# A graph network kernel on one core: the column norms are masked by GpSimd, and VectorE's scaling and mask become one operation

## The chip, the cores and the metric

The kernel runs on one core of a Trainium2 chip. The metric is the device time of one execution, in microseconds (us); lower is better. The median of three runs of the kernel before is 1269.06 us (1268.77 to 1270.68).

## What is computed

The reference, cut to what matters here (128 graphs of 128 nodes with 512 features; `adj` is a 128 by 128 matrix of zeros and ones with ones on its diagonal):

```python
h = relu(layernorm(x))
z_l, z_g, v = h @ W_lang.T, h @ W_grav.T, h @ W_V.T
zn  = z_l / max(norm(z_l), EPS)
A_l = max(zn @ zn.T, 0) * not_eye
A_g = exp(-d2(z_g) / (2 * sigma**2)) * not_eye
K   = w_l * rows_sum_to_one(A_l * adj) + (1 - w_l) * rows_sum_to_one(A_g * adj)
x   = x + (K @ v) @ W_O.T
h   = relu(layernorm(x))
x   = x + (adj * adj).T @ h + bias        # per graph, over the nodes
```

In the second layer the nodes are mixed by the elementwise square of `adj`, and a bias is added to every row. What matters for the change is `A_l`: each raw similarity S[n, m] is multiplied by the reciprocal norm of column m, cut off at zero, and multiplied by mask[n, m] = adj[n, m] without the diagonal. The row's own norm comes in later, in the row factors.

## The kernel before, in words

The 128 graphs are taken in 32 groups of four (`GB` = 4). Every engine has its own instruction stream, and the streams are tied by semaphores; within an engine the order is the one written out in its `iteration` function. Nothing reorders it: an engine that waits holds back everything behind it. All products are made of three passes over high and low parts of fp32 numbers, so for each operand ScalarE writes a high part (`y_hi`, `v_hi`, `h_hi`, `hT_hi`) and VectorE or GpSimd subtracts it to get the low part (`y_lo`, `v_lo`, `h_lo`, `hT_lo`).

One iteration i of TensorE is, in order: eight y blocks (products of the turned h with `Lw`, into four PSUM banks called `ring` used in turn), with the transposes of K of group i-1 before the eighth (L879); four K times v products of group i-1; four P products (`p_ps`); four v products, with the transposes of P after the third (L939); and four second-layer products of group i-1, each of three matmuls (`ring<-h_hi,A_hi`, `h_lo,A_hi`, `h_hi,A_lo`), each of which waits for its `h_lo` (`h2_split`). A product may only start when the bank it writes has been drained (`free`).

VectorE's iteration (`iteration` of the vector block): low parts of the eight y blocks, and between them the mask of the second similarity (`mask_g`), the row factors (L602 to L611), the block transposes of the next h, `combine` and `kt_lo` (L622) of group i-1; then the residual additions and statistics (L631, L637, L568), the squared norms (`squared_norms`, L753, L757 and last L759, which writes `sqc`); then for b = 0 to 3 the low part of v (L557) and that of the turned h of the next group (`turned_lo`, L576), with the sum L744 after b = 2; then the four outputs of group i-1 (L688), which free the ring banks for the next y blocks; then `similarities` (L586: the sums times the column norms) and `mask_l` (L592: cut off at zero, times the mask).

GpSimd's iteration: the ten small operations of `norm1(i+1)` (L277 to L291); `add_bias` of group i-1 for b = 0 and 1 (L301); `norm2(i-1)` (the same ten lines); `add_bias` for b = 2 and 3; `row_norms(i)` (L314 writes `rn` from `sqc`, L316 writes `wr`); and `h2_lo(i-1)` for b = 0 to 3 (L308, writes `h_lo`, after ScalarE's `h_hi`).

SyncE waits for the first operation of `row_norms` and then issues two transfers (`spread_norms`): L214 writes `rn` to a small DRAM tensor, and when that has landed L216 reads it back to all partitions as `rn_cols`, 128 x (128 x 4), with the group's four graphs innermost. VectorE reads it with m innermost, which is a step of four elements.

The last group (i = 31) has no `spread_norms`; its column norms come through PSUM (`r_ps`).

Of the kernel before, what the change touches and what calls it, by code (L numbers as in the profile page):

```python
# [5 lines left out]
ALU = mybir.AluOpType  # L6
# [5 lines left out]
P = 128  # L12
Q = 32
GB = 4
# [6 lines left out]
def gnn_pair(nc, x, adj, w_lang, w_grav, w_v, w_o, gate_logit, log_sigma, bias, out):  # L21
# [6 lines left out]
    LN_STEPS = 10  # L28
    LAST_STEPS = 7
    RN_STEPS = 2  # L30
    blk = {ac: n for n, ac in enumerate(TRI)}
    NQ = P // Q
    TURN = 16 * NQ * NQ
# [20 lines left out]
    with ExitStack() as ctx:  # L54
# [3 lines left out]
        def sem(name):  # L58
            return ctx.enter_context(nc.semaphore(name))
# [10 lines left out]
        P_sb, diag, A = (chain[:, n] for n in range(3))  # L70
# [9 lines left out]
        mask = sb("mask", [P, P])  # L80
# [17 lines left out]
        rn_cols = sb("rn_cols", [P, P, GB])  # L98
# [24 lines left out]
        r_ps = ctx.enter_context(nc.psum_tensor("r_ps", [P, GB, P], F32))  # L123
        kt_ps = ctx.enter_context(nc.psum_tensor("kt_ps", [P, GB, P], F32))

        def bank(use):
# [12 lines left out]
        rn_stored, rn_spread = sem("rn_stored"), sem("rn_spread")  # L139
# [6 lines left out]
        pt_done, r_done, kt_done, kv_done, l1_done = (  # L146
            sem("pt_done"), sem("r_done"), sem("kt_done"), sem("kv_done"), sem("l1_done"))
# [8 lines left out]
        s_ready = sem("s_ready")  # L156
        sq_ready = sem("sq_ready")
        a_ready = sem("a_ready")
# [10 lines left out]
        h2_done = sem("h2_done")  # L169
        x2b_ready = sem("x2b_ready")  # L170
        diag_ready = sem("diag_ready")
        rn_step = sem("rn_step")

        def passes(hi_lo_lhs, hi_lo_rhs):

# [24 lines left out]
        def _(sp):  # L200
# [10 lines left out]
            def spread_norms(g):  # L211

                sp.wait_ge(rn_step, RN_STEPS * g + 1)
                sp.dma_start(rn_dram, rn[:, 0]).then_inc(rn_stored, 16)  # L214
# [47 lines left out]
        def _(pool):  # L262
# [34 lines left out]
            def add_bias(g, b):  # L297
                if b == 0:
                    wait_for(pool, out_stored, 16 * GB * g)
                pool.wait_ge(bn2_done, GB * g + b + 1)  # L300
                pool.tensor_tensor(x_out[:, b], x_rows(g, b), bias_sb[:, :], ALU.add).then_inc(x2b_ready, 1)  # L301

            def norm2(g):
                std_factors(g, bn2, bn2_done, ln2, ln2_step)

# [5 lines left out]
            def row_norms(g):  # L311
                pool.wait_ge(sq_ready, 3 * g + 3)
                wait_for(pool, k_ready, g)
                pool.tensor_tensor(rn[:, 0], sqc[:, :], neg_half[:, :], ALU.pow).then_inc(rn_step, 1)  # L314
                pool.wait_ge(rn_step, RN_STEPS * g + 1)
                pool.tensor_tensor(wr[:, :, :], rn_lg, w8[:, :, :], ALU.mult).then_inc(rn_step, 1)  # L316

            def iteration(i, before=True, after=True):
                if after:
                    norm1(i + 1)  # L320
                if before:
                    for b in range(GB // 2):
                        add_bias(i - 1, b)
                    norm2(i - 1)
                if not after:
                    row_norms(i)
                if before:
                    for b in range(GB // 2, GB):
                        add_bias(i - 1, b)
                if after:  # L330
                    row_norms(i)
                if before:
                    for b in range(GB):
                        h2_lo(i - 1, b)

            norm1(0)
# [7 lines left out]
            g = NG - 1  # L344
# [205 lines left out]
        def _(dve):  # L550
# [25 lines left out]
                dve.tensor_tensor(hT_columns(1, b), h_columns(b), part(hT_columns(0, b)), ALU.subtract)\  # L576
                   .then_inc(ht_lo, 1)

            def similarities(g, last=False):
                if last:  # L580
                    dve.wait_ge(r_done, 1)
                else:
                    dve.wait_ge(rn_spread, 16 * g + 16)
                dve.wait_ge(s_ready, g + 1)
                by_col = r_ps[:, :, :] if last else rn_cols[:, :, :].rearrange("p m b -> p b m")
                dve.tensor_tensor(A[:, :, 0], A[:, :, 0], by_col, ALU.mult).then_inc(a_ready, 1)  # L586

            maskb = mask[:, :].unsqueeze(1).to_broadcast([P, GB, P])

            def mask_l(g):  # L590
                dve.wait_ge(a_ready, 3 * g + 1)
                dve.scalar_tensor_tensor(out=A[:, :, 0], in0=A[:, :, 0], scalar=0.0, in1=maskb,  # L592
                                         op0=ALU.max, op1=ALU.mult).then_inc(a_ready, 1)

# [3 lines left out]
                                         op0=ALU.min, op1=ALU.mult).then_inc(a_ready, 1)  # L598

            def row_factors(g):  # L600
                dve.wait_ge(a_ready, 3 * g + 3)
                dve.tensor_reduce(deg[:, 0], A, AX.X, ALU.add).then_inc(deg_step, 1)  # L602
                dve.wait_ge(deg_step, 5 * g + 1)
                dve.tensor_tensor(deg[:, 1], deg[:, 0], rn_lg, ALU.mult).then_inc(deg_step, 1)
                dve.wait_ge(deg_step, 5 * g + 2)
                dve.tensor_scalar(deg[:, 1], deg[:, 1], EPS, None, ALU.max).then_inc(deg_step, 1)
                dve.wait_ge(deg_step, 5 * g + 3)
                dve.reciprocal(deg[:, 2], deg[:, 1]).then_inc(deg_step, 1)
                dve.wait_ge(deg_step, 5 * g + 4)
                dve.wait_ge(rn_step, RN_STEPS * (g + 1))  # L610
                dve.tensor_tensor(deg[:, 3], deg[:, 2], wr[:, :, :], ALU.mult).then_inc(deg_step, 1)  # L611
# [69 lines left out]
            def h2_lo(g, b):  # L681
                dve.wait_ge(h2_hi, GB * g + b + 1)
                dve.tensor_tensor(h2[1][:, b], h2f[:, b], part(h2[0][:, b]), ALU.subtract).then_inc(h2_split_dve, 1)
# [6 lines left out]
            def iteration(i, before=True, after=True, stats=True):  # L690
                n = 0
                hi = first_hi(i)
                for a in range(C):
                    for l in range(2):
                        hi = hi + 1
                        lo(y[1][:, a, :, l], bank(n).rearrange("p (b m) -> p b m", b=GB), y[0][:, a, :, l], hi)\
                            .then_inc(drained, 1)
                        n += 1
                        if not before and n <= 2:
                            factor_lo(C + 2 * n - 2)  # L700
                            factor_lo(C + 2 * n - 1)
                        if before and n == 1:
                            mask_g(i - 1)
                        if before and n == 2:
                            row_factors(i - 1)
                        if after and n == 4:
                            turn_blocks(i + 1, 0)
                            turn_blocks(i + 1, 1)
                        if before and n == 4:
                            combine(i - 1)  # L710
                        if after and n == 5:
                            turn_blocks(i + 1, 2)
                            turn_blocks(i + 1, 3)
                        if before and n == G_USES - 1:
                            kt_lo(i - 1)
                if before:
                    residual(i - 1, n, first_use(i) + n, i + 2 if stats and after else None)
                else:
                    for c in range(C):
                        hi += 1  # L720
                        lo(MT[1][:, c], bank(n + c), MT[0][:, c], hi).then_inc(drained, 1)
                    x_stats(i + 2, 0, GB)
                n += GB
                if not after:
                    last_chain(i, n, hi)
                    return
                squared_norms(i)
                for b in range(GB):
                    hi = hi + 1
                    lo(v[1][:, b], bank(n), v[0][:, b], hi)\  # L730
                        .then_inc(drained, 1 if before or b < GB - 1 else 1 + GB)
                    n += 1
                    turned_lo(i + 1, b)
                    if b == 2:
                        sum_s(i)
                if before:
                    for b in range(GB):
                        output(i - 1, b, n + b)
                similarities(i)
                mask_l(i)  # L740

            def sum_s(g):
# [18 lines left out]
            def last_chain(i, n, hi):  # L761
                squared_norms(i)

                def v_lo(b):
                    lo(v[1][:, b], bank(n + b), v[0][:, b], hi + b + 1).then_inc(drained, 1)

                v_lo(0)
                sum_s(i)
                similarities(i, last=True)
                mask_l(i)  # L770
                mask_g(i)
                row_factors(i)
                for b in range(1, GB - 1):
                    v_lo(b)
                combine(i)
                v_lo(GB - 1)
                for b in range(GB):
                    output(i - 1, b, n + GB + b)
                    if b == 0:
                        kt_lo(i)  # L780
# [61 lines left out]
            g = NG - 1  # L842
# [165 lines left out]
```

## Time and profile before

| | us |
|---|---|
| median of 3 runs | 1269.06 |
| profiled execution, its own time | 1269.61 |
| its span, first to last instruction | 1267.7 |
| TensorE busy | 1241.2 (98%) |
| VectorE busy | 1058.5 (83%) |
| ScalarE busy | 694.5 (55%) |
| GpSimd busy | 574.7 (45%) |
| granted TensorE clock, mean | 0.996 of full |

In the profile PE is TensorE, DVE is VectorE, ACT is ScalarE, POOL is GpSimd and SPq is SyncE's queue. The shares are means over the span; which wait ends last in a stretch has to be read from the timeline. A matmul's record is longer than the distance to the next matmul, because they are pipelined.

### The profile page before, as it was taken

The numbers are of one execution on the slowest core, as the hardware profiler recorded it, in microseconds if no ns is written. First come the engines' busy times: TensorE is split into PE (matmuls) and PEld (weight loads), VectorE is DVE, ScalarE is ACT, GpSimd is POOL, SyncE is SP. The second block draws the span as 40 slices with busy tenths as digits, with TensorE's granted clock in tenths as the row PEclk, the third lists the DMA queues.
The fourth block names the chain that finished last, engine by engine and source line by source line (L and its number), as shares of the span: only waits on it lengthen the run. The fifth ranks groups of instructions, "written<-read, shape, count | busy, mean of one in ns | idle before, by whom it ended". The sixth has DMA issues, their size and how long they took to land.

```text
span 1267.7 us, 22572 instructions
## 1 busy us (share of the span) xinstructions
PE 1241.2 (98%) x6324; PEld 1039.6 (82%) x6324; DVE 1058.5 (83%) x1826; ACT 694.5 (55%) x1324; POOL 574.7 (45%) x964
## 2 busy tenths in 40 slices
PE   7999999999999999999999999999999999999996
PEld 6878888888888888888888888888888888888884
DVE  5678888988888988888898888898888898888777
ACT  5346555456645456655446655546655545654543
POOL 1115553434554434554434555444555443455433
PEclk9999999999999999999999999999999999999998
DMA  6232424342333343333343232344242444243201
GB/s 243 34 72 81 106 54 95 99 108 81 102 71 78 99 108 87 95 79 70 99 108 97 86 93 56 99 108 103 79 108 49 99 101 108 79 103 69 47 34 66
DMA packets 308894, 112.55 MB, mean 89 GB/s; under 512 B 269840, under 2 KB 269968, under 8 KB 308880
## 3 DMA queue, kind: packets, MB, share of 16 engines
q1 hardware_dynamic: 177360, 95.78, 27.2%
q10 hardware_dynamic: 131520, 16.60, 7.9%
q8 instruction: 7, 0.11, 0.0%
q14 instruction: 7, 0.06, 0.0%
HBM read 46.20 MB, written 33.62 MB: 63 GB/s over the span
## 4 chain that ended last, share of the span: by engine, by line
PE 93%; DVE 4%; ACT 1%; issue 1%; DMA 1%; POOL 0%; SPq 0%; DVEq 0%; ACTq 0%
PE ring L866 75%; PE p_ps L866 15%; PE p_ps L939 2%; PE kt_ps L879 1%; DMA h2f<-in_L_gnn_W_grav 1%; DVE x_out L688 0%; DVE bn L568 0%; DVE y_lo L557 0%; ACT h L379 0%; DVE bn L637 0%; DVE x_ring L631 0%; DVE y_lo L784 0%; DVE deg L602 0%; DVE v_lo L784 0%; DVE hT_lo L557 0%
## 5 line engine op out<-in xcount | busy, mean ns | idle before, releaser
L301 POOL TENSOR_TENSOR x_out<-x_ring,bias_sb 128x512 f32<-128x512 f32 x128 | 162.8, 1295 | 499.9 <-DVE bn L637 499.9
L866 PE MATMUL ring<-hT_hi,Lw_hi 128*128 128x512 f32 x640 | 256.9, 401 | 4.9 <-DVE hT_lo L576 2.1
L406 ACT ACTIVATE y_hi<-ring 128x512 fp32r<-128x512 f32 x256 | 148.3, 592 | 206.5 <-PE ring L866 203.7
L866 PE MATMUL ring<-hT_hi,Lw_lo 128*128 128x512 f32 x640 | 250.6, 392 | 0.0
L866 PE MATMUL ring<-hT_lo,Lw_hi 128*128 128x512 f32 x640 | 250.2, 391 | 0.0
L866 PE MATMUL ring<-MT_hi,hT_hi 128*128 128x512 f32 x512 | 203.0, 396 | 0.0
L557 DVE TENSOR_TENSOR v_lo<-ring,v_hi 128x512 fp32r<-128x512 f32 x128 | 88.5, 692 | 136.8 <-ACT v_hi L442 136.8
L866 PE MATMUL ring<-MT_hi,hT_lo 128*128 128x512 f32 x512 | 200.0, 391 | 0.0
L866 PE MATMUL ring<-MT_lo,hT_hi 128*128 128x512 f32 x512 | 199.9, 390 | 0.0
L308 POOL TENSOR_TENSOR h_lo<-h2f,h_hi 128x512 fp32r<-128x512 f32 x124 | 158.0, 1296 | 84.8 <-ACT h_hi L476 84.8
L557 DVE TENSOR_TENSOR y_lo<-ring,y_hi 128x512 fp32r<-128x512 f32 x256 | 169.2, 680 | 28.4 <-ACT y_hi L406 28.3
L430 ACT ACTIVATE chain<-p_ps 128x512 f32<-128x512 f32 x64 | 38.2, 598 | 240.5 <-PE p_ps L866 240.5
L866 PEld LDWEIGHTS ring<-hT_hi,Lw_hi 128*128 128x128 f32 x640 | 120.2, 188 | 44.0 <-DVE x_out L688 10.7
L866 PE MATMUL p_ps<-y_hi,hT_lo 128*128 128x256 f32 x512 | 145.2, 284 | 0.0
L866 PE MATMUL p_ps<-y_lo,hT_hi 128*128 128x256 f32 x512 | 145.2, 284 | 0.0
L866 PE MATMUL p_ps<-y_hi,hT_hi 128*128 128x256 f32 x512 | 145.0, 283 | 0.0
L866 PEld LDWEIGHTS ring<-hT_hi,Lw_lo 128*128 128x128 f32 x640 | 120.2, 188 | 26.4
L866 PEld LDWEIGHTS ring<-hT_lo,Lw_hi 128*128 128x128 f32 x640 | 120.5, 188 | 21.8
L469 ACT ACTIVATE h2f<-x_ring,ln 128x512 f32 (+1 forms) x128 | 100.5, 809 | 49.6 <-POOL ln L291 40.0
L866 PEld LDWEIGHTS ring<-MT_hi,hT_lo 128*128 128x128 f32 x512 | 96.2, 188 | 20.6
L866 PEld LDWEIGHTS ring<-MT_lo,hT_hi 128*128 128x128 f32 x512 | 96.5, 188 | 17.9
L866 PEld LDWEIGHTS ring<-MT_hi,hT_hi 128*128 128x128 f32 x512 | 96.4, 188 | 18.0
(160 smaller groups left out, 2537.0 us busy)
## 6 DMA issues: line engine op xcount, KB each, us to landing
x_ring<-in_x SPq DMA_DIRECT2D x32, 1024.0 KB, 5.5
out<-x_out SPq DMA_DIRECT2D x128, 256.0 KB, 2.2
h_turned<-h SPq DMA_DIRECT2D x248, 64.0 KB, 2.1
h_turned<-h ACTq DMA_DIRECT2D x248, 64.0 KB, 2.1
rn_cols<-rn_dram SPq DMA_DIRECT2D x31, 256.0 KB, 3.9
x_ring<-in_L_gnn_W_lang SPq DMA_DIRECT2D x4, 256.0 KB, 5.6
h2f<-in_L_gnn_W_grav SPq DMA_DIRECT2D x1, 1024.0 KB, 9.2
chain<-in_L_gnn_W_O SPq DMA_DIRECT2D x1, 1024.0 KB, 13.0
```

Of the source, the lines that this page charges most:

```text
L301: pool.tensor_tensor(x_out[:, b], x_rows(g, b), bias_sb[:, :], ALU.add).then_inc(x2b_ready, 1)
L308: pool.tensor_tensor(h2[1][:, b], h2f[:, b], h2[0][:, b].bitcast(F32), ALU.subtract)\
L406: act.activation(y[0][:, a, :, l], bank(n).rearrange("p (b m) -> p b m", b=GB), ACT.Copy)\
L430: act.activation(P_sb[:, 2 * half:2 * half + 2], p_ps[:, 2 * half:2 * half + 2], ACT.Copy)\
L469: act.activation(h2f[:, b], x_rows(g, b), ACT.Relu, bias=ln2[:, SHIFT, b:b + 1], scale=ln2[:, RSTD, b:b + 1]).then_inc(h2_done, 1)
L557: return dve.tensor_tensor(out, ps, part(hi), ALU.subtract)
L866: mm = pe.matmul(out, lhsT, rhs, start=(k == 0), stop=(k == len(terms) - 1))
L879: mm = pe.transpose(kt_ps[:, b], K[:, b], ident[:, :])
L939: mm = pe.transpose(p_ps[:, k // 2, k % 2], P_sb[:, k // 2, k % 2], ident[:, :])
```

## The change

`mask_norms(g)` is new on GpSimd: it waits until `rn_cols` of the group has landed and multiplies it by the mask in place (4 graphs innermost, so the mask is read with a step of zero there). On VectorE `similarities` is gone, and `mask_l` does the cut at zero and the multiplication by the masked norms in one operation. GpSimd's order changes: `row_norms(i)` goes ahead of the second pair of `add_bias`, `h2_lo` for b = 0 and 1 follows that pair, then `mask_norms(i)`, then `h2_lo` for b = 2 and 3. The last group keeps the two operations, in a function of their own, and its GpSimd order.

```diff
+            def mask_norms(g):
+                pool.wait_ge(rn_spread, 16 * g + 16)
+                by_col = mask[:, :].unsqueeze(2).to_broadcast([P, P, GB])
+                pool.tensor_tensor(rn_cols[:, :, :], rn_cols[:, :, :], by_col, ALU.mult).then_inc(rn_masked, 1)
+
...
-                if not after:
-                    row_norms(i)
+                row_norms(i)
                 if before:
                     for b in range(GB // 2, GB):
                         add_bias(i - 1, b)
+                    for b in range(GB // 2):
+                        h2_lo(i - 1, b)
                 if after:
-                    row_norms(i)
+                    mask_norms(i)
                 if before:
-                    for b in range(GB):
+                    for b in range(GB // 2, GB):
                         h2_lo(i - 1, b)
...
-            def similarities(g, last=False):
...
-                dve.tensor_tensor(A[:, :, 0], A[:, :, 0], by_col, ALU.mult).then_inc(a_ready, 1)
...
             def mask_l(g):
-                dve.wait_ge(a_ready, 3 * g + 1)
+                dve.wait_ge(rn_masked, g + 1)
+                dve.wait_ge(s_ready, S_STEPS * (g + 1))
+                dve.scalar_tensor_tensor(out=A[:, :, 0], in0=A[:, :, 0], scalar=0.0,
+                                         in1=rn_cols[:, :, :].rearrange("p m b -> p b m"),
+                                         op0=ALU.max, op1=ALU.mult).then_inc(a_ready, 1)
...
             def row_factors(g):
-                dve.wait_ge(a_ready, 3 * g + 3)
+                dve.wait_ge(a_ready, 2 * g + 2)
...
-                similarities(i)
                 mask_l(i)
```

## Rows read from the trace of the kernel before

**Rows 1.** The page: busy time of each engine, share of the span, instructions.

```profile
PE 1241.2 (98%) x6324; PEld 1039.6 (82%) x6324; DVE 1058.5 (83%) x1826; ACT 694.5 (55%) x1324; POOL 574.7 (45%) x964
```

**Rows 2.** Waits, whole span: who waited for whom, us in total, times, longest.

```profile
PEld ring L866 <- issue: 16.9, 31, 2.5
```

**Rows 3.** Timeline of PE in one iteration: start us, us, instruction, count.

```profile
617.33 0.39 PE L866 MATMUL ring<-hT_hi,Lw_lo 128*128 128x512 f32 x1
617.79 0.49 PE L866 MATMUL ring<-v_hi,KT_hi 128*128 128x512 f32 x1
618.12 0.39 PE L866 MATMUL ring<-v_lo,KT_hi 128*128 128x512 f32 x1
...
640.25 0.39 PE L866 MATMUL ring<-h_hi,A_hi 128*128 128x512 f32 x1
...
641.02 0.50 PE L866 MATMUL ring<-hT_hi,Lw_hi 128*128 128x512 f32 x1
```

**Rows 4.** Timeline of DVE in the same iteration; in brackets the idle time before.

```profile
604.94 1.07 DVE L586 TENSOR_TENSOR chain<-chain,rn_cols 128x512 f32<-128x512 f32 x1
...
606.65 0.68 DVE L557 TENSOR_TENSOR y_lo<-ring,y_hi 128x512 fp32r<-128x512 f32 x1
...
616.98 0.67 DVE L622 TENSOR_TENSOR KT_lo<-kt_ps,KT_hi 128x512 fp32r<-128x512 f32 x1
618.39 0.69 DVE L557 TENSOR_TENSOR y_lo<-ring,y_hi 128x512 fp32r<-128x512 f32 x1 [0.73 <-ACT y_hi L406]
...
626.22 0.67 DVE L753 TENSOR_TENSOR chain<-chain,diag_of 128x512 f32<-128x512 f32 x1
...
628.97 0.69 DVE L759 TENSOR_SCALAR sqc<-sq 128x4 f32<-128x4 f32 x1
...
631.17 0.68 DVE L576 TENSOR_TENSOR hT_lo<-h_turned,hT_hi 128x512 fp32r<-128x512 f32 x1
...
634.38 0.82 DVE L576 TENSOR_TENSOR hT_lo<-h_turned,hT_hi 128x512 fp32r<-128x512 f32 x1
...
636.09 0.68 DVE L576 TENSOR_TENSOR hT_lo<-h_turned,hT_hi 128x512 fp32r<-128x512 f32 x1
...
639.04 0.69 DVE L557 TENSOR_TENSOR v_lo<-ring,v_hi 128x512 fp32r<-128x512 f32 x1 [1.14 <-ACT v_hi L442]
639.65 0.72 DVE L576 TENSOR_TENSOR hT_lo<-h_turned,hT_hi 128x512 fp32r<-128x512 f32 x1
640.29 2.47 DVE L688 TENSOR_TENSOR x_out<-ring,x_out 128x512 f32<-128x512 f32 x4
```

**Rows 5.** Timeline of POOL in the same iteration; the row at 633.35 is the second of its pair.

```profile
604.11 0.20 POOL L287 TENSOR_TENSOR ln<-ln 128x4 f32<-128x4 f32 x1
...
626.23 0.72 POOL L287 TENSOR_TENSOR ln<-ln 128x4 f32<-128x4 f32 x1
...
628.34 2.55 POOL L301 TENSOR_TENSOR x_out<-x_ring,bias_sb 128x512 f32<-128x512 f32 x2
630.83 1.04 POOL L314 TENSOR_TENSOR rn<-sqc,neg_half 128x4 f32<-128x4 f32 x1
...
632.10 2.56 POOL L308 TENSOR_TENSOR h_lo<-h2f,h_hi 128x512 fp32r<-128x512 f32 x2
...
633.35 1.31 POOL L308 TENSOR_TENSOR h_lo<-h2f,h_hi 128x512 fp32r<-128x512 f32 x1
...
637.27 2.55 POOL L308 TENSOR_TENSOR h_lo<-h2f,h_hi 128x512 fp32r<-128x512 f32 x2 [2.61 <-ACT h_hi L476]
```

**Rows 6.** DMA issues, whole span: queue, count, KB each, median us to landing.

```profile
rn_cols<-rn_dram SPq DMA_DIRECT2D x31, 256.0 KB, 3.9
...
rn_dram<-rn SPq DMA_DIRECT2D x31, 2.0 KB, 1.4
```

**Rows 7.** Timeline of DVE in the first group.

```profile
63.34 0.17 DVE L759 TENSOR_SCALAR sqc<-sq 128x4 f32<-128x4 f32 x1
```

**Rows 8.** Timeline of POOL in the first group.

```profile
63.59 1.01 POOL L314 TENSOR_TENSOR rn<-sqc,neg_half 128x4 f32<-128x4 f32 x1 [27.03 <-DVE sqc L759]
```

More of the change, by code:

```diff
@@ L30, in gnn_pair @@
     RN_STEPS = 2
+    S_STEPS = 1
     blk = {ac: n for n, ac in enumerate(TRI)}
@@ L171, in gnn_pair @@
         diag_ready = sem("diag_ready")
-        rn_step = sem("rn_step")
+        rn_step, rn_masked, a_scaled = sem("rn_step"), sem("rn_masked"), sem("a_scaled")
         def passes(hi_lo_lhs, hi_lo_rhs):
@@ L577, in turned_lo, with mask_l_last @@
                    .then_inc(ht_lo, 1)
-            def similarities(g, last=False):
[L580 to L585, printed above, removed]
-                dve.tensor_tensor(A[:, :, 0], A[:, :, 0], by_col, ALU.mult).then_inc(a_ready, 1)
             maskb = mask[:, :].unsqueeze(1).to_broadcast([P, GB, P])
             def mask_l(g):
-                dve.wait_ge(a_ready, 3 * g + 1)
+                dve.wait_ge(rn_masked, g + 1)
[3 more added lines that the diff above has]
+                                         op0=ALU.max, op1=ALU.mult).then_inc(a_ready, 1)
+            def mask_l_last(g):
+                dve.wait_ge(r_done, 1)
+                dve.wait_ge(s_ready, S_STEPS * (g + 1))
+                dve.tensor_tensor(A[:, :, 0], A[:, :, 0], r_ps[:, :, :], ALU.mult).then_inc(a_scaled, 1)
+                dve.wait_ge(a_scaled, 1)
                 dve.scalar_tensor_tensor(out=A[:, :, 0], in0=A[:, :, 0], scalar=0.0, in1=maskb,
@@ L768, in last_chain @@
                 sum_s(i)
-                similarities(i, last=True)
-                mask_l(i)
+                mask_l_last(i)
                 mask_g(i)
```

## The prediction

> **What bounds the kernel now.** I read the page first: TensorE is busy 98% of the span [rows 1]. VectorE, from which the change takes work, is busy 83%, and GpSimd, which gets it, 45% [rows 1]. From shares one would call the change harmless and nearly useless. So the question is what is left of TensorE's idle time, and who ends it. The waits [rows 2] name one place that comes 31 times, once a group, with 16.9 us of idle time in all, whose end the profile puts down to "issue". The timeline of TensorE [rows 3] places it. At 617.33 the last matmul of the y blocks starts and the next one, the first of K times v, only at 617.79, where the pace is 0.23 us; VectorE's low part of K ends at 616.98 + 0.67 = 617.65 [rows 4], 0.14 before the start, so this is the true releaser. The matmul after that comes 0.33 later, not 0.23. The stall is thus 0.23 + 0.10 = 0.33 us. A second place is the head of the y blocks, 641.02, just after the first output is drained: 640.29 + 0.68 = 640.97 (four outputs take 2.47, so 0.60 each after the first of 0.68) [rows 3, 4].
>
> Two things are then to be seen in the other engines' timelines. VectorE has no idle time from 604.94 until after the low part of K, so work taken from it there brings that forward; after it VectorE waits for ScalarE (618.39, bracket), which waits for TensorE, and its timing from there on hangs on TensorE's y blocks alone [rows 4]. And GpSimd and VectorE hold each other up. The small sqc operation takes 0.17 in the first group, where GpSimd is waiting for it [rows 7, 8]; here it takes 0.69: it starts at 628.97 and ends at 629.66, when GpSimd's first bias sum (628.34 plus about 1.29) ends [rows 4, 5]. The low part of turned h at 634.38 takes 0.82 and not 0.68: GpSimd's operation ends at 633.35 + 1.31 = 634.66, VectorE's at 635.20, 0.54 later. In the other direction, a GpSimd operation on 128x4 that started at 626.23, beside VectorE's L753 (626.22 to 626.89), took 0.72 and ended 0.06 after it; the same line in norm1 took 0.20 [rows 4, 5]. Operations of VectorE that read PSUM (L557, L688) show none of this.
>
> **The change, part by part.**
>
> *VectorE's operation that goes.* From the start of L586 to the next y_lo are 1.71 us (604.94 to 606.65) for the two operations [rows 4]. The fused one reads the same rn_cols with the same step of four elements, so I take the 1.07 of L586; the row does not exclude the 0.69 of the operation without that step, nor 1.07 plus a few hundredths. VectorE saves about 0.6 us an iteration. The low part of K then ends near 617.05, before TensorE's 617.56, and the stall of 0.33 goes. What is late next decides its worth. TensorE comes 0.33 earlier to its last v product, ScalarE's v_hi and VectorE's v_lo start at 638.71 and not 639.04, and the last turned low part (L576) wants to start at 639.32. But it reads two operands in SBUF, and GpSimd's last h_lo runs until 637.27 + 2.55 = 639.82. By the 0.54 above it ends at 640.36, the first output at 640.96, where it ended at 640.97. So without any change on GpSimd, the 0.33 is given back at the next y block: gain 0.0 us.
>
> *Row norms moved ahead of two bias sums.* With the row norms next, GpSimd only waits from 628.34 on, so sqc is not held up: 628.97 + 0.17 = 629.14. L314 starts 0.08 later (63.51 to 63.59 [rows 7, 8]), at 629.22, and SyncE's L214 about 1.05 later, at 630.27, 1.6 us earlier than now. Then 1.4 and 3.9 us to the landings [rows 6]: rn_cols is there at 635.6 to 636.1. SyncE itself has nothing else queued there: its outputs and x loads wait for later events. The first bias sum of the pair starts at 629.22 + 1.27 = 630.49 (L314 to the next long operation is 1.27, 630.83 to 632.10 [rows 5]).
>
> *The new operation on GpSimd.* No row shows a multiplication there with a step of zero. The nearest rows are 128x512 sums of 1.29 us, at a pitch of 1.25 [rows 5]; I take 1.29. Above, VectorE's ratio for its strided operand, 1.07 to 0.69, would give 2.0 us; below, 1.25.
> The Trainium skill (GPSIMD Engine Reference, section 7, Performance pitfalls) puts a surcharge of about half on GpSimd reads whose step exceeds 8 bytes. The steps here are 4 and 0 bytes, so the page speaks for 1.29; no row shows it.
>
> *Price of a collision.* When VectorE wants an operation of two SBUF operands during a long GpSimd operation, it starts 0.14 before that one's end is recorded and ends 0.54 after it. The next GpSimd operation then starts 0.14 before VectorE's end, so 0.40 after its predecessor's end, and not 0.04 before it (632.10 + 1.29 against 633.35 [rows 5]): 0.44 us for each collision. In the trace of before every collision falls on the last operation of a GpSimd pair, with idle time behind it, so nothing is lost. After the change GpSimd has seven long operations in a row:
>
> - bias sum 2: 630.49 to 631.78; turned low part 0 wants 631.17: collision
> - bias sum 3: 632.18 to 633.47
> - h_lo 0: 633.43 to 634.72; turned low part 1 wants 634.38: collision
> - h_lo 1: 635.12 to 636.41; turned low part 2 wants 636.09: collision
> - mask of the norms: 636.81 to 638.10 (rn_cols is there, no wait for it)
> - h_lo 2: 638.06 to 639.35; turned low part 3 wants 639.32, at its very end
> - h_lo 3: if VectorE gets in first, 639.75 to 641.04; if not, 639.31 to 640.60.
>
> TensorE wants h_lo 3 at 640.25, less the 0.33 [rows 3]. In the first branch it starts 0.14 after 641.04, loses 0.11 at the restart and takes 3 x 0.227: the y blocks are in pace at 641.97. Before, that was 641.02 + 0.11 = 641.13. So +0.84 an iteration. In the second branch h_lo 3 allows 641.53, but turned low part 3 ends at 640.60 + 0.54 = 641.14, the first output at 641.74, the y blocks are in pace at 641.90: +0.77. I take 0.81. norm1 on GpSimd, behind h_lo 3, is then 0.8 to 1.3 us later, against y blocks that are 0.8 later too; its first reader is ScalarE after the third y_hi, so I cost it at nothing. If that cover were gone, up to 0.5 us an iteration would come on top.
>
> *The sum.* mask_norms runs for 31 groups, with h_lo behind it in 30: 30 x 0.81 = 24.3 us. The first group has no h_lo behind its mask, and the last keeps its order: 0. The profiled execution is 1269.61 with a span of 1267.7, 0.04% above the median of 1269.06: 1269.1 + 24.3 = 1293.4 us.
>
> At this place a page can be weighed. The rows give 0.44 for a collision. The Trainium skill (SBUF — State Buffer, The single rule and Practical consequences) says that the shared port pair is held for the whole instruction by whichever starts first, and that the other fully blocks. By that a collision would cost GpSimd a full operation of VectorE. The trace agrees that they block, but its blocked operations end 0.54 and not 0.68 after the other.
>
> **The rivals.**
>
> *Not slower (12%).* GpSimd is not delayed by VectorE when its next long operation is already queued; only short operations show such a delay now. Then the row is 630.49, 631.74, 632.99, 634.24 to 635.53, the mask 635.65 to 636.94, and h_lo 2 and 3 start at 637.27 after ScalarE as now: 1269 us, since the 0.33 is given back as worked out. It decides at a mask ending by 637.3. Against it: sqc, wanted at 628.97, got in between two long operations [rows 4, 5].
>
> *Faster (8%).* As the last, and turned low part 3 is not held up either: first output at 640.60, h_lo 3 at 639.82, y blocks in pace at 640.07 + 0.68 = 640.75, so 0.38 less an iteration, 1257.7 us. Against it stands the 0.82 of the low part at 634.38 [rows 4].
>
> *One collision fewer (12%).* The mask ends at 637.66, h_lo 3 at 640.16, turned low part 3 at 640.70, the first output at 641.30 against 640.97: +0.33 x 30, 1279 us. The ends lie 0.3 us from the collisions' edges, so this is possible.
>
> *A longer mask or longer holds (18%).* With 2.0 us for the mask, h_lo 3 ends at 641.74 and the y blocks are in pace at 642.67: +1.54 x 30, 1315 us. With 0.68 a collision (VectorE's usual duration, at 631.17 [rows 4]), three cost 0.72 more: h_lo 3 ends about 641.8, 1316 us.
> The second of these is what the rule on the shared port pair (the Trainium skill, SBUF — State Buffer) would give.
>
> **How the numbers follow.** The forecast's own case has 50%, by its rows of 1290 to 1298 us. Slower cases together 80%, unchanged 12%, faster 8%. A measurement of this kernel tells 0.2% (2.5 us) from no change. The range goes from the unchanged case to the longer mask: 1268 to 1316 us; it leaves out the faster case and what a still slower mask would bring.
>
> **What would show it.** Right: L759 at 0.17 us; L214 about 12 us after the eighth y_lo; KT_lo no longer the releaser of K times v; the low parts L576 at 0.9 to 1.3 us for b = 0 to 2; TensorE waiting for POOL h_lo in 30 iterations, 1 us or so each; a period of 38.55 and not 37.74. Wrong: h_lo 2 still waiting for ScalarE's h_hi, the mask beginning after a long wait for the DMA, or L301 and L308 unstretched while L576 is.

## The result, and the profile after

The changed kernel takes 1285.2 us (median of 4 runs, 1284.56 to 1285.99) against 1269.1 us for the kernel before on the same chip: ratio 1.0125, interval 1.0107 to 1.0142, slower by 16.1 us. The profiled execution took 1285.48 us, with a span of 1283.7. The forecast was 1293.4, in a range of 1268 to 1316.

The page of the changed kernel, busy time by engine, answers to [rows 1]. VectorE's busy time went up by 12 us although it has 31 operations fewer, and GpSimd's by 73 us for 31 more of about 1.1 us each, 34 us of work. The rest is time in which the two engines hold each other up: the profile counts an instruction as busy while it is held, as the longer records below show. So a busy share that rose is not work that was added.

```profile
PE 1248.2 (97%) x6324; PEld 1040.5 (81%) x6324; DVE 1070.9 (83%) x1795; ACT 691.7 (54%) x1324; POOL 647.8 (50%) x995
```

The waits of the whole span, against [rows 2]: who waited for whom, us in total, times, longest. The stall that the profile calls issue comes 59 times and not 31. It has also moved: before K times v it is gone, and it now stands before the second-layer products of b = 2 and b = 3 (the weight loads ahead of them wait 0.34 and 0.72 us on average). And there is a new line: TensorE waits for GpSimd's h_lo once in nearly every group.

```profile
PEld ring L872 <- issue: 33.0, 59, 2.5
PEld ring L872 <- DVE x_out L696: 16.1, 29, 0.6
...
PE ring L872 <- POOL h_lo L314: 9.3, 31, 0.8
```

TensorE's timeline in one iteration, against [rows 3] (start us, us, instruction, count). The K times v products now begin 0.23 after the last y product, at 626.12: that stall is gone. The second-layer products for b = 2 and 3, at 609.60 and 610.84, do not follow at the pace of 0.68 but 1.24 apart, and the y blocks start 0.52 after the last matmul.

```profile
609.29 0.39 PE L872 MATMUL ring<-h_hi,A_lo 128*128 128x512 f32 x1
609.60 0.49 PE L872 MATMUL ring<-h_hi,A_hi 128*128 128x512 f32 x1
...
610.84 0.49 PE L872 MATMUL ring<-h_hi,A_hi 128*128 128x512 f32 x1 [0.29 <-POOL h_lo L314]
...
611.40 0.40 PE L872 MATMUL ring<-h_hi,A_lo 128*128 128x512 f32 x1
611.92 0.50 PE L872 MATMUL ring<-hT_hi,Lw_hi 128*128 128x512 f32 x1
...
625.89 0.39 PE L872 MATMUL ring<-hT_hi,Lw_lo 128*128 128x512 f32 x1
626.12 0.39 PE L872 MATMUL ring<-v_hi,KT_hi 128*128 128x512 f32 x1
```

GpSimd's timeline from there to the next head, against [rows 5]. Both pairs of long operations now take 3.00 us and not 2.55, and the mask 1.56.

```profile
637.69 1.01 POOL L320 TENSOR_TENSOR rn<-sqc,neg_half 128x4 f32<-128x4 f32 x1 [0.87 <-DVE sqc L766]
...
638.97 3.00 POOL L302 TENSOR_TENSOR x_out<-x_ring,bias_sb 128x512 f32<-128x512 f32 x2
641.93 3.00 POOL L314 TENSOR_TENSOR h_lo<-h2f,h_hi 128x512 fp32r<-128x512 f32 x2
644.89 1.56 POOL L307 TENSOR_TENSOR rn_cols<-rn_cols,mask 128x512 f32<-128x512 f32 x1
646.41 2.53 POOL L314 TENSOR_TENSOR h_lo<-h2f,h_hi 128x512 fp32r<-128x512 f32 x2
```

VectorE's timeline of the same time, against [rows 4]. sqc is down to 0.17 us; the four turned low parts (L583) take 1.17, 0.91, 0.91 and 1.67 us where they took 0.68, 0.82, 0.68 and 0.72; and the first output, 649.42 to 650.11, is again what the next y block waits for. The last low part is the one that matters most: wanted at 647.83, while h_lo 3 runs until 648.94, it ends at 649.50.

```profile
637.44 0.17 DVE L766 TENSOR_SCALAR sqc<-sq 128x4 f32<-128x4 f32 x1
...
639.64 1.17 DVE L583 TENSOR_TENSOR hT_lo<-h_turned,hT_hi 128x512 fp32r<-128x512 f32 x1
...
642.87 0.91 DVE L583 TENSOR_TENSOR hT_lo<-h_turned,hT_hi 128x512 fp32r<-128x512 f32 x1
...
644.57 0.91 DVE L583 TENSOR_TENSOR hT_lo<-h_turned,hT_hi 128x512 fp32r<-128x512 f32 x1
...
647.83 1.67 DVE L583 TENSOR_TENSOR hT_lo<-h_turned,hT_hi 128x512 fp32r<-128x512 f32 x1
649.42 2.47 DVE L696 TENSOR_TENSOR x_out<-ring,x_out 128x512 f32<-128x512 f32 x4
651.81 1.06 DVE L591 SCALAR_TENSOR_TENSOR chain<-chain,rn_cols 128x512 f32<-128x512 f32 x1
```

The heads of the y blocks stand at 611.92 and 650.15: a period of 38.23 us, where it was 37.74 (603.28 to 641.02). Over the 28 periods from the second to the last but one the means are 38.25 and 37.75, so 0.50 each and 13.9 of the 16.0 us between the two spans. The first period is 2.4 us longer, of which some 1.6 come from TensorE's clock (last section), and the last one 0.1; the first y blocks after the start come 0.35 us earlier.

### The profile page after: what moved, and what is told of

It reads as the page before. It is cut to its first block, busy times and chain, and to the rows that moved or that the text cites. A ratio compares the mean times of both kernels' runs of the same rounds, so it can differ in the third digit from the quotient of the medians.

```text
span 1283.7 us, 22545 instructions
## 1 busy us (share of the span) xinstructions
PE 1248.2 (97%) x6324; PEld 1040.5 (81%) x6324; DVE 1070.9 (83%) x1795; ACT 691.7 (54%) x1324; POOL 647.8 (50%) x995
## 4 chain that ended last, share of the span: by engine, by line
PE 86%; issue 5%; DVE 5%; ACT 2%; DMA 1%; POOL 0%; DVEq 0%; SPq 0%; ACTq 0%
PE ring L872 69%; PE p_ps L872 14%; PE p_ps L945 2%; DVE x_out L696 2%; ACT v_hi L449 2%; PE kt_ps L885 1%; DMA h2f<-in_L_gnn_W_grav 1%; DVE bn L575 0%; DVE v_lo L564 0%; ACT h L386 0%; DVE bn L645 0%; DVE x_ring L639 0%; DVE y_lo L790 0%; DVE v_lo L790 0%; DVE hT_lo L564 0%
## 5 line engine op out<-in xcount | busy, mean ns | idle before, releaser
L302 POOL TENSOR_TENSOR x_out<-x_ring,bias_sb 128x512 f32<-128x512 f32 x128 | 176.4, 1400 | 489.8 <-DVE bn L645 489.8
L314 POOL TENSOR_TENSOR h_lo<-h2f,h_hi 128x512 fp32r<-128x512 f32 x124 | 171.1, 1401 | 5.9 <-ACT h_hi L483 5.9
L872 PEld LDWEIGHTS ring<-hT_hi,Lw_hi 128*128 128x128 f32 x640 | 120.5, 188 | 46.1 <-DVE x_out L696 16.1
L583 DVE TENSOR_TENSOR hT_lo<-h_turned,hT_hi 128x512 fp32r<-128x512 f32 x124 | 141.9, 1144 | 0.0
```

The costliest lines, as they stand in the source:

```text
L314: pool.tensor_tensor(h2[1][:, b], h2f[:, b], h2[0][:, b].bitcast(F32), ALU.subtract)\
L872: mm = pe.matmul(out, lhsT, rhs, start=(k == 0), stop=(k == len(terms) - 1))
```

## The experiments

All times are medians beside runs of the kernel before on the same chip; in brackets the ratio to it with its 95% interval. The kernel before has medians from 1269.1 to 1270.5 us on the chips used, so times of different experiments compare to about 1.5 us.

**Do the collisions make the loss? Two kernels, one edit.** The low part of turned h is given a PSUM tile as its first operand, so that VectorE's instruction has only one operand in SBUF. It computes other values; nothing else changes. It was put into the changed kernel (e3) and into the kernel before (e4).

```diff
-                dve.tensor_tensor(hT_columns(1, b), h_columns(b), part(hT_columns(0, b)), ALU.subtract)\
+                dve.tensor_tensor(hT_columns(1, b), kt_ps[:, :, :], part(hT_columns(0, b)), ALU.subtract)\
```

> The changed kernel, but the low part of turned h (L583) reads its first operand from PSUM (kt_ps) in place of SBUF (h_turned), so that VectorE's operation has one SBUF operand; the values of hT_lo are then others. Theory (collisions with GpSimd's long operations are the loss): the pairs of bias sums and of h_lo take 2.55 and not 3.00 us, L583 takes 0.68, h_lo 2 starts when ScalarE's h_hi is there, the first output ends 1.0 us earlier than in the changed kernel, period 37.2 us, time 1253 to 1258 us. Rival (the loss is the mask operation itself or its wait for the DMA, not the collisions): 1280 us or more.

> The same edit in the kernel before (the low part of turned h reads PSUM in place of h_turned; other values). Theory: every collision there falls on the last operation of a GpSimd pair and costs nothing but 0.04 us at the last low part: 1267 to 1269 us. Rival (reading PSUM is by itself faster on the path, or the collisions already cost time before): 1264 us or less, and then the run of the changed kernel with this edit proves less.

e3: 1256.9 us (0.9893, 0.9878 to 0.9908). e4: 1267.5 us (0.9982, 0.9973 to 0.9992). The same edit takes 28 us from the changed kernel and 2 from the kernel before. With it in both, the change is a gain of 11 us. GpSimd's timeline in e3:

```profile
626.06 2.56 POOL L302 TENSOR_TENSOR x_out<-x_ring,bias_sb 128x512 f32<-128x512 f32 x2
628.56 2.56 POOL L314 TENSOR_TENSOR h_lo<-h2f,h_hi 128x512 fp32r<-128x512 f32 x2
631.32 1.11 POOL L307 TENSOR_TENSOR rn_cols<-rn_cols,mask 128x512 f32<-128x512 f32 x1 [0.20 <-DMA rn_cols<-rn_dram]
632.85 2.54 POOL L314 TENSOR_TENSOR h_lo<-h2f,h_hi 128x512 fp32r<-128x512 f32 x2 [0.42 <-ACT h_hi L483]
```

The pairs are back at 2.55, the mask waits for its DMA and the last pair for ScalarE: without the collisions the new order fits into the iteration. The collisions are the cause of the loss. The edit frees both engines at once, so it does not tell GpSimd's lateness from the hold of VectorE's last low part.

**What is the mask operation worth, and the order?** e5 leaves mask_norms out of the changed kernel and lets VectorE wait for the landed norms; the language mask is left out of the computation. e2 does the same with GpSimd in its order of before.

```diff
-                if after:
-                    mask_norms(i)
...
-                dve.wait_ge(rn_masked, g + 1)
+                dve.wait_ge(rn_spread, 16 * g + 16)
```

> The changed kernel in its new GpSimd order, without mask_norms: VectorE's fused operation waits for the landed norms and multiplies by the unmasked ones, so the language mask is left out. Theory: two collisions remain but the pair of h_lo 2 and 3 waits for ScalarE's h_hi again; turned low part 3 is held up by h_lo 3 until 0.67 us before where it is now; period 37.56, time 1263 to 1267 us, so 0.67 of the 1.7 us that the mask and its collision occupy are on the path. Rival (GpSimd's order itself costs time): 1275 us or more.

> GpSimd exactly as in the kernel before, no mask_norms; on VectorE only the fused operation (on unmasked norms: the language mask is left out). It prices VectorE's saved 0.6 us alone. Theory: the stall before K times v goes, but turned low part 3 is then held up by h_lo 3 and gives most of it back: 0.1 to 0.17 us an iteration gained, 1264 to 1267 us. Rival (VectorE's saved time is worth the whole stall, 0.33 us or more an iteration): 1259 us or less.

e5: 1266.5 us (0.9973, 0.9963 to 0.9983). e2: 1265.9 us (0.9973, 0.9963 to 0.9984). Both as the theory had them. The two orders differ by 0.6 us, so the order costs nothing by itself; the mask operation where the change puts it is worth some 19 us (1.0125 against 0.9973). VectorE's saved 0.6 us an iteration (some 19 us in all) is worth 3 to 4 us of time. VectorE's timeline in e2 shows who takes the rest: the last turned low part, wanted at 637.44, takes 1.04 us and not 0.68, because h_lo 3 runs until 637.93.

```profile
636.83 0.69 DVE L563 TENSOR_TENSOR v_lo<-ring,v_hi 128x512 fp32r<-128x512 f32 x1 [0.83 <-ACT v_hi L448]
637.44 1.04 DVE L582 TENSOR_TENSOR hT_lo<-h_turned,hT_hi 128x512 fp32r<-128x512 f32 x1
```

**The order by itself.** e6 is the kernel before with the new GpSimd order, without the mask operation, and nothing else; e7 is the changed kernel with row_norms back behind the bias sums.

```diff
-                if not after:
-                    row_norms(i)
+                row_norms(i)
                 if before:
                     for b in range(GB // 2, GB):
                         add_bias(i - 1, b)
-                if after:
-                    row_norms(i)
...
```

(e6; the rest of its edit splits the loop of h_lo in two and leaves their order as it was. e7 moves the row norms back in the changed kernel, and its mask_norms stays between h_lo 1 and h_lo 2.)

> The kernel before with the new GpSimd order alone (row norms ahead of the second bias sums, h_lo 0 and 1 behind them), no mask_norms, both VectorE operations as before. Theory: two collisions in four long operations, but the pair of h_lo 2 and 3 still waits for ScalarE, so nothing reaches TensorE: 1268 to 1270.5 us. Rival (the order itself costs time): 1275 us or more.

> The changed kernel with one part undone: row_norms runs behind the second pair of bias sums, as before; mask_norms stays between h_lo 1 and h_lo 2. Theory (a chain from sqc over the DMA to h_lo 3, worked out from rows): sqc is held up again (0.69 us), rn_cols lands near 637.1 to 637.5 on the clock of the kernel before, the mask ends near 638.4, h_lo 3 near 641.2, y blocks in pace at 642.1: 1.0 us an iteration more than before, 1294 to 1302 us. Rival (moving the row norms costs collisions and brings nothing): 1285 us or less.

e6: 1269.7 us (0.9997, 0.9988 to 1.0006). Its timeline has the two pairs of 3.00 us, and the last pair still waits 0.83 for ScalarE: collisions with slack behind them cost nothing. e7: 1301.3 us (1.0251, 1.0235 to 1.0267), 16 us above the changed kernel. There GpSimd stands still until the norms have landed, 2.84 us in this iteration:

```profile
613.61 1.10 POOL L307 TENSOR_TENSOR rn_cols<-rn_cols,mask 128x512 f32<-128x512 f32 x1 [2.84 <-DMA rn_cols<-rn_dram]
614.66 2.98 POOL L314 TENSOR_TENSOR h_lo<-h2f,h_hi 128x512 fp32r<-128x512 f32 x2
```

So moving the row norms ahead was a needed part of this change, and worth 16 us of it.

**Where else could the mask stand?** e1 keeps the fused operation and the order of before, with mask_norms as GpSimd's last operation of the iteration.

```diff
                 if before:
                     for b in range(GB):
                         h2_lo(i - 1, b)
+                if after:
+                    mask_norms(i)
```

> The fused VectorE operation and mask_norms, but on GpSimd the order of before with mask_norms as the last operation, behind h_lo 3; all outputs as in the reference. Theory: h_lo 2 and 3 come as before, the saved VectorE time brings what it brought without the mask (about 0.1 us an iteration), and norm1 of the next group comes 1.3 us later, which ScalarE's normalisation feels by up to 1 us and TensorE by 0 to 0.25 us: 1265 to 1273 us. Rival (the mask operation costs its time wherever it stands on GpSimd): 1280 us or more.

e1: 1266.6 us (0.9965, 0.9952 to 0.9979), with nothing left out of the computation: the whole idea of the change, some 20 us faster than the changed kernel by the ratios and 0.35% faster than the one before. Here the turned low part, wanted at 638.98, is already waiting when h_lo 3 ends at 639.43, and goes ahead of the mask: it takes 1.00 us, and the mask 1.56 for its 1.11.

e8 adds a new order on ScalarE, so that h_lo 3 is done before the last turned low part is wanted; e9 has that order alone.

```diff
+                        h2_copy(i - 1, 2)
                         h2_full(i - 1, 3)
-                        h2_copy(i - 1, 2)
                         h2_copy(i - 1, 3)
```

> As e1_mask_last, and on ScalarE the copy h_hi 2 goes ahead of the normalisation h2f 3. Theory: h_lo 2 starts 0.7 us earlier, h_lo 3 ends near 639.25 on the clock of the kernel before, so turned low part 3 (wanted at 639.2) is hardly held up and the saved VectorE time is kept: first output near 640.4, y blocks in pace near 640.6 and not 641.13; 1253 to 1261 us. Rival (something else holds the head of the y blocks): within 2 us of e1_mask_last.

> The kernel before with only the ScalarE order of e8 (the copy h_hi 2 ahead of the normalisation h2f 3), no mask_norms and both VectorE operations. Theory (e8 lost its time because turned low part 3, wanted 0.18 us after GpSimd had begun the mask, waited for the whole of it): without a mask there is nothing to wait for, the last turned low part comes at 639.65 as before, 1267 to 1270 us. Rival (the ScalarE order itself costs the time that e8 lost): 1280 us or more.

e8: 1281.0 us (1.0086, 1.0072 to 1.01). This expectation was wrong by 20 us and more. GpSimd's timeline in e8:

```profile
605.28 2.66 POOL L314 TENSOR_TENSOR h_lo<-h2f,h_hi 128x512 fp32r<-128x512 f32 x2 [1.92 <-ACT h_hi L484]
607.90 1.11 POOL L307 TENSOR_TENSOR rn_cols<-rn_cols,mask 128x512 f32<-128x512 f32 x1
```

VectorE's timeline in e8, the last turned low part:

```profile
608.08 1.47 DVE L584 TENSOR_TENSOR hT_lo<-h_turned,hT_hi 128x512 fp32r<-128x512 f32 x1
```

h_lo 3 ended in time, but then the mask began at 607.90, 0.18 us before VectorE wanted its low part, and held it up to 0.54 us past its own end. I had cleared one long operation from that place and put the next one into it. e9 at 1269.9 us (0.9994, 0.9985 to 1.0003) shows that ScalarE's order costs nothing.

**The mask out of the way.** e10 is e8 with mask_norms behind norm1 of the next iteration, and VectorE's fused operation behind mask_g there; e11 is e10 without ScalarE's new order; e12 is e10 with both of VectorE's masks behind the second y_lo.

```diff
                 if after:
                     norm1(i + 1)
                 if before:
+                    mask_norms(i - 1)
...
-                        if before and n == 1:
-                            mask_g(i - 1)
                         if before and n == 2:
+                            mask_g(i - 1)
+                            mask_l(i - 1)
                             row_factors(i - 1)
```

(e12; in e10 and e11 the two calls stand at n == 1.)

> As e8, but mask_norms of a group runs behind norm1 of the next iteration and VectorE's fused operation behind mask_g there, so that no long GpSimd operation is on when turned low part 3 is wanted; the mask falls beside VectorE's work at the head of the y blocks, which has 1 us or more to spare. Outputs as in the reference. Theory: turned low part 3 takes 0.7 us and not 1.47, the first output ends 0.8 us earlier than in e8, period 37.2 to 37.3 us, 1254 to 1260 us. Rival (something else holds the head of the y blocks, or the late mask holds back K): 1264 us or more.

> As e10 with ScalarE's order of before, so that h_lo 3 still runs when turned low part 3 is wanted. Theory: that low part is held up by h_lo 3 to the end of it, as in e1 and e2, and the time is theirs, 1264 to 1268 us. Rival (e10's gain comes from moving the mask, not from the free port): within 2 us of e10.

> As e10, but VectorE runs mask_g and the fused operation behind the second y_lo and not the first, so that while GpSimd masks the norms VectorE is at a low part that reads PSUM. Outputs as in the reference. Theory (e10 fell short because mask_g, with two SBUF operands, was held up 0.48 us by GpSimd's mask, and that came back as a stall before K times v): mask_g takes 0.7 and not 1.17 us, KT_lo is no longer late, period 37.2 to 37.35 us, 1254 to 1258 us. Rival (e10's rest is something else): 1261 us or more.

e10: 1262.3 us (0.9944, 0.993 to 0.9958), 2 us above its expectation. e11: 1280.8 us (1.0085, 1.0071 to 1.0099), a miss by 13 us. e12: 1257.9 us (0.9911, 0.9894 to 0.9927), the fastest of the kernels that leave nothing out.

What fell short in e10 and e11 is to be seen at VectorE's head of the iteration: one row of e10, one of e11, one of e12.

```profile
601.80 1.17 DVE L605 SCALAR_TENSOR_TENSOR chain<-chain,mask 128x512 f32<-128x512 f32 x1
```

```profile
612.31 1.10 DVE L591 SCALAR_TENSOR_TENSOR chain<-chain,rn_cols 128x512 f32<-128x512 f32 x1 [1.00 <-POOL rn_cols L307]
```

```profile
600.18 0.77 DVE L605 SCALAR_TENSOR_TENSOR chain<-chain,mask 128x512 f32<-128x512 f32 x1
```

In e10 mask_g was wanted while GpSimd masked the norms and took 1.17 us for 0.69. With that 0.48 there is again a stall before K times v, of 0.06, and a slow restart of 0.10. In e12 it takes 0.77 and no such stall is left: 4.3 us less than e10. In e11, counted from the head of the y blocks, norm1 is later and the mask starts 0.6 us later than in e10. VectorE's mask_g now comes just ahead of it (0.70), so that it is the mask that is held up: 1.55 us and not 1.11. The fused operation waits 1.00 us for it in each iteration, and TensorE then waits for y_lo 59 times. The hold that the theory of e11 was about did not come: the last turned low part takes 0.74 us there. The theory looked only at the end of the iteration and left out the wait for the mask.

## Why the prediction was right

The direction, the place of the loss and its mechanism came as forecast. The size did not come as well: 24.3 us were forecast and 16.1 measured, and 1285.2 lies below the rows of 1290 to 1298 us that the prediction gave its own case. By the number alone the rival of one collision fewer (1279) is 6 us away and the forecast 8; it is the rows that decide for the forecast's case. Nearly all terms that were off made the forecast too large. The other way went only 0.04 us an iteration and what the slower clock of the first group added, up to 1.6 us in all, which nobody had forecast: that much of the agreement is luck.

By its own steps, on the clock of one iteration, counted from the head of the y blocks (603.28 in the forecast, 611.92 in the trace, so 8.64 us are taken off the trace's times):

| | forecast | measured |
|---|---|---|
| L759/L766 sqc, duration | 0.17 | 0.17 |
| row norms start (L314/L320) | 629.22 | 629.05 |
| bias sum 2 starts | 630.49 | 630.33 |
| h_lo 0 starts | 633.43 | 633.29 |
| the mask ends | 638.10 | 637.81 |
| h_lo 3 ends (second branch) | 640.60 | 640.30 |
| first output ends | 641.74 | 641.47 |
| y blocks start (before: 641.02) | 641.79 | 641.51 |

*The stall before K times v* went, as forecast, and *was given back* at the head of the y blocks: by e2, 3 to 4 us of about 10 remained. The forecast said 0.0 an iteration; about 0.1 was right. VectorE's whole later chain is 0.17 us earlier, against a prediction that let it hang on the y blocks alone: 0.08 stands already at the eighth y_lo (618.39 before, 618.31 on the same clock now), and the rest has come by the end of the third residual addition (620.96 and 620.79). That is the gap of the second row of the table. The prediction also read the 16.9 us of "issue" as one place once a group: the longest of the 31, of 2.5 us, is the pause of the first group. Its sum does not use that figure.

*The collisions* came where forecast: three in the row, each at 0.45 us (3.00 less 2.55) against 0.44, and the fourth in the second of the two branches. The rows show the blocked operation ending 0.54 to 0.56 us after the other. Of the two readings that the prediction weighed, the shared port pair held for the whole instruction (the Trainium skill, SBUF — State Buffer, Who interferes with whom, the single rule) against 0.44 from the rows, the rows' price decided. That whoever is first holds up the other agrees with the trace for the long operations; the time lost is less than the other's recorded duration of 0.68. Why is not shown. It does not hold for every GpSimd instruction: the power on 128x4 at 630.83 (L314, 1.04 us) [rows 5] also reads SBUF, and the turned low part that starts inside it, at 631.17, takes its free 0.68 [rows 4].

*The mask operation* was mis-sized: 1.11 us where it runs free (e3, e8), 1.29 forecast. In the table the gap to the forecast grows by 0.15 us from the start of h_lo 0 to the end of the mask. So the term of 0.81 was 0.49 because of 0.17 (VectorE's chain), 0.15 (the mask) and 0.04 (the mean of two branches, of which the cheaper came true), less some 0.04 that the other rows lost again.

*Moving the row norms*: L215 at 638.73 (630.09 on the forecast's clock, forecast 630.27), and the mask did not wait for the landing, except in two of the 31 groups. The prediction gave the move no price; e7 does: 16 us more without it.

*The first group* was costed at 0; the slower clock in the profiled execution is worth some 1.6 us there. The last full iteration, costed like the others, has 0.1. *The rivals*: a mask ending by 637.3 would have been unchanged; it ended at 637.81. One collision fewer is excluded by the records: 0.45 us more in each of the two pairs and in the mask (1.56 for 1.11). The faster case, 1257.7, is what e3 shows without collisions (1256.9). GpSimd undelayed by VectorE is excluded by the 3.00 us pairs. The range was wide on the upper side for a mask of 2.0 us that did not come.

## What to carry to other kernels

Work moved from VectorE to GpSimd is not moved to a free engine. In these traces each long GpSimd operation is a time in which VectorE's instructions with two SBUF operands wait, and so did the small sqc with its one (0.69 for 0.17); in a row of long GpSimd operations each such instruction also pushes back the rest of the row. Count the slack behind the row, not the engine's busy share, and place long GpSimd operations beside VectorE's reads of PSUM, as e12 does. The same idea went from +1.3% to -0.35% by its place on GpSimd alone (e1), and to -0.9% with the orders of ScalarE and VectorE fitted to it (e12). When one blocker is taken from a critical place, look what the queue puts there next (e8), and who waits for the thing that was moved (e11).

## What the runs showed of the hardware that was not expected

**TensorE's clock after a short pause.** In the first group TensorE stands still for 2.13 us before the y blocks, in the kernel before and in the changed one. In five of the fourteen profiled executions (the changed kernel, e1, e3, e8 and e9) the granted clock is then about 0.5 of full, the lower of its two levels (1.2 and 2.4 GHz); in the changed kernel this lasts about 3.4 us. In the other nine it stays full. The windows view of the same 2 us, first the kernel before and then the changed one (us, busy time and count of PE, PEld, DVE, ACT and POOL, granted clock, DMA share, GB/s):

```profile
76.00:78.00 2.00, 2.00 (x11) 1.64 (x10) 1.91 (x4) 1.20 (x2) 0.00 (x0) 1.00 0.03 8
```

```profile
76.00:78.00 2.00, 2.00 (x6) 1.59 (x5) 1.54 (x3) 1.03 (x2) 0.00 (x0) 0.51 0.00 0
```

Six matmuls run there and not eleven; the first seven y blocks of that group, up to the transposes, take 12.6 us (from 74.80) and not 11.0 (from 75.15), so 1.6 us. e9, without any mask on GpSimd, shows it in its profiled execution (0.50 in the same window), and e7 and e12, which have the mask, do not, so it does not come with the change. The runs of e9 fall into two sets, near 1268.5 and near 1270.2 us, 1.7 apart, and those of the kernel before likewise, near 1269 and 1271; that these sets are the same pause with and without the drop fits the numbers, but was only seen in the profiled executions. What decides it was not tried.

**VectorE gets in between two queued GpSimd operations.** Where a VectorE instruction is already waiting when a long GpSimd operation ends, it goes ahead of the next one: in the pairs of 3.00 us it ends 0.54 to 0.56 after the first of the pair, and it is the record of the second that is 0.45 longer (h_lo 1: 1.76 for 1.30).

**A small GpSimd operation did not hold VectorE up.** GpSimd's power on 128x4 takes 1.04 us. The turned low part that starts inside L314 0.7 to 0.8 us before its end took 0.68 in all 30 iterations of the kernel before, and so did the second L753 (0.68 to 0.69) inside L289. So the length of a GpSimd record alone does not say whether it blocks. What decides it was not tried.

**A strided operand.** VectorE's fused operation takes 1.06 us with `rn_cols` read at a step of four elements, and 0.69 with an operand without that step. GpSimd's multiplication with the mask read at a step of zero takes 1.11, less than its plain sum (1.29). The operation, the step and the writing in place differ together there, and which of them makes it was not tried.
